# One Trainium2 core, two cross-attention and feed-forward layers: entry into cross attention reordered, opening of linear attention reordered with its row loads in pieces, expert ranks from float16 zeros and ones

## The chip, the cores and the metric

The kernel runs on one core of one Trainium2 chip, in one launch. The metric is the device time of that core in microseconds. Three runs of the kernel before gave 390.52, 391.15 and 392.76 us; their median is 391.15 us. A core has a matrix engine (PE, with its weight load PEld), a vector engine (DVE), a scalar engine (ACT), a general engine (POOL), and SP, which here only issues DMAs. Each works off its own list of instructions in order, and they meet at semaphores. Sums of matmuls stand in PSUM, in eight banks; everything else is in SBUF.

## The reference

Inputs are `x` (32 batches of 64 tokens of 256 numbers: 2048 tokens), a context of the same shape and a mask. Four parts follow each other, each added to `x`:

```python
x = x + _L0_xattn_ref(_layernorm(x), ctx_2048, Wq, Wg, bg, Wkv, Wo)      # linear attention, 16 heads
x = x + _L0_ffn_ref(_layernorm(x), gate_w, ..., se_gate_w)               # 2 of 8 experts, and a shared one
x = x + _L1_xattn_ref(_layernorm(x), ctx_2048, mask, Wq, bq, ..., residual_scale)   # softmax cross attention
x = x + _L1_ffn_ref(_layernorm(x), W0, bias0, W1, bias1)                 # dense feed-forward with gelu
```

Linear attention: `q`, `k` pass through `x+1` or `exp(x)`, `kv_summary = k^T v` and `k_sum` are made per batch and head, and `out = (q kv_summary / (q k_sum) * sigmoid(x Wg + bg)) Wo`. The expert part takes the two best of 8 scores per token, mixes those experts' outputs and adds a gated shared expert. Cross attention makes keys and values of the context, scores, a clipped and masked softmax, the weighted values, an output product and a layer norm of the result.

## The kernel before

The 2048 tokens are 16 tiles of 128. Many products are made from pairs of rounded numbers, a high part (`w0h`, `xTh`, written by ACT) and a low part (`w0l`, `xTl`, the rest, written by DVE or POOL), with three matmuls for one product (`product`, L334 to L336).

**Linear attention** goes in slots, one for a tile, written out by hand for each engine in a `slot0` of its own; an engine's order in a slot is the order of the lines there, and what belongs to other tiles is put in with a distance (`s.tile(2)` is the tile two ahead). On PE a slot holds the key and value product of its tile (L334 to L336, 512 wide), the attention of the tile before (L1924), for even tiles the queries of a pair, the gate product with the bias row (L1990), the product of keys and values (L2004), the transposition of the normed tile two ahead (L375), and the output of the tile two behind. The normed tile comes from ACT (`norm`, L873), which needs the rsqrt that POOL makes for a pair of tiles (`pair_rstd`), which needs the moments that DVE makes (`moments`, L1234 and L1236). Tiles 0 and 1 are normed by DVE ahead of the first slot.

**The opening** is what stands ahead of these slots and slots 0 and 1. SP issues the loads in a written order: rows 0 and 1 of `x` by tiles, the context of tile 0, the layer's weights in pieces (`W0_AT`), the gate's bias, rows of tiles 2 and 3, and so on; the rows of tiles 6 to 15 are one load of 1280 KB. ACT and DVE split each piece of weights (`split_hi`, L840, and `split_w0`, L1189). DVE then writes the two parts of the bias row (`bias_parts`, L1196 and L1198), for which PE's gate product of slot 0 waits, and then the moments of tiles 2 and 3. The expert weights come 482 columns at a time into two buffers in `raw`; ACT rounds them at the end of each slot (`weights_hi_step`, L470), POOL takes the rest (`weights_lo_step`, L482), and the load of piece t waits for POOL's step of piece t - 2.

**Ranks.** A token's place in the list of its expert is its rank among the tokens that chose the expert. For four tiles at a time (`rank_members`, L1897 to L1903) PE multiplies a triangle of ones (`below`) and full squares of ones (`ones`) with `member`, which holds 0 or 1 for each token and expert, all in float32.

**Entry into cross attention.** PE makes keys and values for 8 pairs of context tiles: `keys(p)` and `values(p)`, 12 matmuls each. ACT writes the keys out (`keys`, four instructions, L1027), DVE the values (`values`, L1626), into buffers by head. PE's `values(p)` waits until DVE has written `values(p - 2)`, since they share a bank. Meanwhile POOL fetches the two expert rows of each token (`gather`, L753), two indirect DMAs for a tile; DVE adds them to `x` and takes the moments (`entering`: L1662, L1668, L1675, L1679), POOL makes the rsqrt (`joint_rstd`, L766 to L773), ACT norms (`norm_x`, L1053), PE transposes (L2222) and ACT copies (`normed_in`, L1074). After that come slots again (`slot2`), in which DVE clips scores (`clip`, L1746), then enters the tile four ahead.

Of the kernel before, what the change touches and what calls it, by code (L numbers as in the profile page):

```python
# [20 lines left out]
F16 = mybir.dt.float16  # L21
# [6 lines left out]
P = 128  # L28
# [110 lines left out]
def build(nc, A, out):  # L139
    xs_d = nc.dram_tensor("xs_rows", (XROWS, D), F32, kind="Internal").ap()  # L140
    ys_d = nc.dram_tensor("ys_rows", (USED * P, D), F32, kind="Internal").ap()
    with ExitStack() as ctx:
        def sb(name, shape, dt=F32):
            return ctx.enter_context(nc.sbuf_tensor(name, shape, dt))
# [60 lines left out]
        below, ones = sb("below", [P, P]), sb("ones", [P, P])  # L205
# [46 lines left out]
        member = raw[:, 2020:2148].rearrange("p (t e) -> p t e", e=EXPERTS)  # L252
# [261 lines left out]
        def _(sp):  # L514
# [7 lines left out]
            for i in range(4):  # L522
                load(raw[:, W0_AT[i]:W0_AT[i + 1]], A["w_l0"][:, W0_AT[i]:W0_AT[i + 1]], w0_in[i])
            load(bg_raw[:, :], A["bg"], const_in)
            load(x[:, 2:4, :], x_d[:, 2:4, :], const_in)
# [21 lines left out]
            load(x[:, 6:TILES, :], x_d[:, 6:TILES, :], x_in[1])  # L547
# [8 lines left out]
            with sp.Fori(1, TILES // 2 - 1) as i:  # L556
                for r in range(2):
                    load_ctx(i * 2 + (2 + r), r)
                    load_w(0, i * 2 + r, r)
# [96 lines left out]
        def _(pool):  # L656
# [34 lines left out]
            def slot0(s):  # L691
                if s.is_at(0):
                    pair_rstd(1)
                if tile := s.tile(-3):
                    route_rstd(tile[0])
                if tile := s.tile(2):
                    ctx_lo_step(pool, *tile)
                if s.ring == 1 and s.tile(4):
                    pair_rstd((s.at + 3) // 2)
                if tile := s.tile(-SCATTER_AFTER):  # L700
                    scatter(tile[0])
                if tile := s.tile(0):
                    weights_lo_step(pool, 0, *tile)
# [100 lines left out]
            for t in range(3):  # L804
                gather(t)
            joint_rstd(0)
            gather(3)
            joint_rstd(1)
# [26 lines left out]
        def _(act):  # L835
# [47 lines left out]
            def slot0(s):  # L883
# [20 lines left out]
                if s.is_at(0):  # L904
                    split_hi(4)
# [12 lines left out]
                if s.is_at(0):  # L918
                    ctx_hi_step(act, 2, 0)
                    norm(2)  # L920
# [8 lines left out]
                if tile := s.tile(0):  # L929
                    weights_hi_step(act, 0, *tile)  # L930
# [158 lines left out]
            normed_in(1)  # L1089
            norm_x(2)  # L1090
            keys(6)
# [88 lines left out]
        def _(dve):  # L1180
# [25 lines left out]
            def route_setup(part):  # L1206

                if part == 0:
                    dve.wait_ge(R["weights_hi"], 1)
                    nc.vector.tensor_tensor(rwl, rw_raw[:, :, :], rwh.bitcast(F32),  # L1210
                                            ALU.subtract).then_inc(R["weights"], 1)
                else:
                    dve.wait_ge(late_in, 16 * 6)
                    dve.wait_ge(R["setup"], 4)
                    nc.vector.tensor_scalar(below[:, :], step[:, :], lane[:, 0:1], None, ALU.is_gt)
                    nc.vector.tensor_tensor(upto8[:, :, :], wide(iota8, 2, EXPERTS), wide(iota8, 1, EXPERTS), ALU.is_ge)
# [34 lines left out]
            split_w0(3)  # L1251
            dve.wait_ge(const_in, 16 * 3)
            bias_parts(bg_raw[:, :], 2)
            for t in range(2, 4):
                moments(t)

# [100 lines left out]
            def slot0(s):  # L1357
# [43 lines left out]
                if s.is_at(2):  # L1401
                    dve.wait_ge(x_in[1], 16)
# [296 lines left out]
            ctx_pair_lo(6)  # L1699
            values(2)  # L1700
            entering(0)
            values(3)
            ctx_pair_lo(7)
            entering(1)
            values(4)
# [148 lines left out]
        def _(pe):  # L1854
# [32 lines left out]
            def rank_members(b, scored):  # L1887
# [14 lines left out]
                for t in range(PER_BATCH - 1):  # L1902
                    last = nc.tensor.matmul(  # L1903
                        rank[:, t + 1:, :], ones[:, :],
# [537 lines left out]
```

## Time and profile before

| | us |
|---|---|
| time of the profiled execution | 391.04 |
| its span, from the first instruction to the last | 389.1 |
| PE busy | 367.5 (94%) |
| DVE busy | 293.6 (75%) |
| ACT busy | 244.7 (63%) |
| POOL busy | 219.8 (56%) |

The span is 1.9 us shorter than the time; that part lies ahead of the first and behind the last instruction. A busy PE is not a PE at its peak, since matmuls are pipelined and a matmul that runs at half clock counts as busy too. The mean granted clock of the span is 0.996 of full speed. In the page's 40 slices of 9.7 us PE is busy over 90% in nearly all of them; the first has 7 tenths.

### The profile page before, as it was taken

What the parts mean: (1) busy time and instruction counts of PE and PEld (TensorE: products, weight loads), DVE (VectorE), ACT (ScalarE), POOL (GpSimd) and SP (SyncE); (2) the same over time, 40 slices, a digit from 0 to 9 for tenths busy, and PEclk for the clock granted to TensorE, in tenths of its full rate; (3) what the DMA queues carried; (4) which work ended last, traced back from release to release, by engine and by line L of the source; (5) the groups of instructions that cost most, each with busy time, mean ns of one, the idle gap of its engine ahead of it and who ended that gap; (6) DMA issues with size and microseconds to landing.
All of it is one profiled execution on the core that took longest, in us unless ns stands there. A gap on an engine that the chain in (4) does not pass through costs nothing.

```text
span 389.1 us, 10016 instructions
## 1 busy us (share of the span) xinstructions
PE 367.5 (94%) x3258; PEld 329.5 (85%) x3258; DVE 293.6 (75%) x842; ACT 244.7 (63%) x563; POOL 219.8 (56%) x370
## 2 busy tenths in 40 slices
PE   7799999998999999999999999799999989999996
PEld 6588888786878888989998999688877869999996
DVE  5689988988988879764544499888889995766533
ACT  4576776575554351467876887777877778644550
POOL 3455576378887674604441677577787886531100
PEclk9899999999999999999999999999999999999999
DMA  7561221121332145549784532121120000010101
GB/s 250 187 203 42 79 66 55 40 93 66 87 116 95 70 177 185 161 136 289 232 272 150 192 86 79 50 62 57 54 57 3 2 3 2 7 50 29 56 27 56
DMA packets 31187, 38.13 MB, mean 98 GB/s; under 512 B 4385, under 2 KB 28322, under 8 KB 31138
## 3 DMA queue, kind: packets, MB, share of 16 engines
q1 hardware_dynamic: 28066, 29.11, 24.4%
q0 software_dynamic: 3072, 8.39, 6.4%
q8 instruction: 28, 0.46, 0.5%
q14 instruction: 21, 0.17, 0.1%
HBM read 24.90 MB, written 12.58 MB: 96 GB/s over the span
## 4 chain that ended last, share of the span: by engine, by line
PE 55%; DVE 19%; POOL 12%; issue 8%; ACT 4%; DMA 1%; SPq 0%; ACTq 0%; POOLq 0%; DVEq 0%
PE PS L334 9%; PE PS L335 8%; PE PS L336 8%; PE PS L2266 8%; PE PS L2284 8%; POOL xs_rows L710 3%; PE PS L2101 2%; POOL wfl L482 2%; POOL rj L769 2%; PE PS L2004 2%; ACT raw L1063 1%; POOL rows_early L753 1%; DVE arena_f L1746 1%; PE PS L2342 1%; POOL sj L773 1%
## 5 line engine op out<-in xcount | busy, mean ns | idle before, releaser
L1102 ACT ACTIVATE arena_f<-PS,cols 128x256 f16<-128x256 f32 x64 | 26.5, 472 | 21.6 <-PE PS L2266 19.1
L334 PE MATMUL PS<-wfh,arena_r 128*128 x117 | 35.1, 300 | 2.2 <-DVE arena_r L1602 1.5
L334 PE MATMUL PS<-w0h,arena_r 128*128 128x256 f32 (+1 forms) x96 | 34.8, 363 | 0.6 <-DVE w0l L1189 0.3
L335 PE MATMUL PS<-wfl,arena_r 128*128 x117 | 33.0, 282 | 0.0
L336 PE MATMUL PS<-wfh,arena_r 128*128 x117 | 32.8, 281 | 0.0
L2266 PE MATMUL PS<-arena_r,w1h 128*128 128x256 f32 x128 | 31.2, 284 | 0.0
L335 PE MATMUL PS<-w0l,arena_r 128*128 128x256 f32 (+1 forms) x96 | 31.1, 324 | 0.0
L2266 PE MATMUL PS<-arena_r,w1l 128*128 128x256 f32 x128 | 31.0, 283 | 0.0
L336 PE MATMUL PS<-w0h,arena_r 128*128 128x256 f32 (+1 forms) x96 | 30.9, 322 | 0.0
L488 POOL TENSOR_TENSOR w1l<-raw,w1h 128x384 fp32r<-128x384 f32 (+1 forms) x14 | 12.7, 910 | 29.8 <-ACT w1h L474 29.8
L710 POOL DMA_INDIRECT xs_rows<-rows_early,posi x24 | 24.2, 1010 | 8.9 <-issue 6.7
L1746 DVE TENSOR_SCALAR arena_f<-PS,lim 128x512 f32<-128x512 f32 x32 | 22.4, 743 | 4.4 <-PE PS L2342 4.3
L1608 DVE SCALAR_TENSOR_TENSOR arena_f<-arena_f,PS 128x256 f32<-128x256 f32 x20 | 8.9, 446 | 21.8 <-ACT arena_f L994 21.8
L2266 PEld LDWEIGHTS PS<-arena_r,w1h 128*128 128x128 f32 x128 | 24.5, 191 | 0.4 <-ACT arena_r L1112 0.4
L334 PEld LDWEIGHTS PS<-wfh,arena_r 128*128 128x128 f32 x117 | 22.0, 188 | 3.2 <-issue 3.2
L2266 PEld LDWEIGHTS PS<-arena_r,w1l 128*128 128x128 f32 x128 | 24.5, 191 | 0.0
L335 PEld LDWEIGHTS PS<-wfl,arena_r 128*128 128x128 f32 x117 | 22.1, 189 | 0.0
L336 PEld LDWEIGHTS PS<-wfh,arena_r 128*128 128x128 f32 x117 | 22.0, 188 | 0.0
L334 PEld LDWEIGHTS PS<-w0h,arena_r 128*128 128x128 f32 x96 | 18.4, 191 | 3.9 <-issue 2.1
L482 POOL TENSOR_TENSOR wfl<-raw,wfh 128x482 fp32r<-128x482 f32 (+4 forms) x18 | 19.2, 1070 | 4.3 <-ACT wfh L470 4.1
L1117 ACT ACTIVATE arena_f<-arena_f 128x1024 f32<-128x1024 f32 x16 | 16.9, 1059 | 4.8 <-DVE arena_f L1746 4.8
L336 PEld LDWEIGHTS PS<-w0h,arena_r 128*128 128x128 f32 x96 | 18.3, 191 | 1.5
(317 smaller groups left out, 1375.4 us busy)
## 6 DMA issues: line engine op xcount, KB each, us to landing
arena_f<-xs_rows SPq DMA_DIRECT2D x39, 128.0 KB, 2.5
ys_rows<-raw SPq DMA_DIRECT2D x19, 256.0 KB, 2.9
raw<-in_w_ffn SPq DMA_DIRECT2D x16, 241.0 KB, 2.7
raw<-in_w_l SPq DMA_DIRECT2D x12, 192.0 KB, 3.1
ctx_raw<-in_ctxT SPq DMA_DIRECT2D x16, 128.0 KB, 2.0
out<-arena_f SPq DMA_DIRECT2D x7, 256.0 KB, 2.1
raw<-in_w_l SPq DMA_DIRECT2D x5, 256.0 KB, 4.4
x<-in_x SPq DMA_DIRECT2D x1, 1280.0 KB, 6.4
```

Source lines behind the costliest of these rows:

```text
L334: nc.tensor.matmul(out_ap, lh, rh, start=first, stop=False)
L335: nc.tensor.matmul(out_ap, lh, rl, start=False, stop=False)
L336: return nc.tensor.matmul(out_ap, ll, rh, start=False, stop=last)
L482: last = nc.gpsimd.tensor_tensor(wfl[part][:, to], raw[:, r * FFN_CHUNK + at.start:r * FFN_CHUNK + at.stop], wfh[part][:, to].bitcast(F32) ...
L488: last = nc.gpsimd.tensor_tensor(w1l[:, to], raw[:, r * FFN_CHUNK + first:r * FFN_CHUNK + L1_CHUNK], w1h[:, to].bitcast(F32), ALU.subtract)
L710: nc.gpsimd.indirect_dma_start(out=xs_d, out_offset=bass.IndirectOffsetOnAxis(posi[:, k, t:t + 1], 0), in_=xn2[t % 8], in_offset=None).the ...
L1102: nc.scalar.activation(md16[:, g % 2, n, :], PS[:, M_H[n // 2], (n % 2) * D:(n % 2 + 1) * D], ACT.Gelu, bias=cols[:, 2 * KC + n:2 * KC + n ...
L1117: nc.scalar.activation(flat, flat, ACT.Exp).then_inc(S2["probs"], 1)
L1608: nc.vector.scalar_tensor_tensor(out=gub[:, j % 2, :, :], in0=gub[:, j % 2, :, :], scalar=2.0, in1=up, op0=ALU.mult, op1=ALU.mult).then_in ...
L1746: nc.vector.tensor_scalar(pp[t % 2][:, b, :, :], PS[:, bank:bank + 2, b * 2 * P:(b + 1) * 2 * P], -50.0, lim[:, 2 * t + b:2 * t + b + 1], ...
L2266: last = nc.tensor.matmul(PS[:, M_H[n // 2], (n % 2) * D:(n % 2 + 1) * D], m0w[w][:, c, n * P:(n + 1) * P], mX[g % 2][:, c, :], start=c + ...
L2284: last = nc.tensor.matmul(out, mD[g % 2][:, n, k * P:(k + 1) * P], m1w[w][:, n, :], start=n + w == 0, stop=n + w == NFF)
```

## The change

It has four parts, told here in the order of the program.

1. **Loads.** The load of the rows of tiles 2 and 3 is issued before the third piece of weights instead of behind the bias, and has a semaphore slot of its own. The one load of tiles 6 to 15 becomes three: tiles 6 and 7 in its place, tiles 8 to 11 behind the third piece of expert weights, tiles 12 to 15 behind the fourth.
2. **Order in the opening.** DVE takes the moments of tiles 2 and 3 before it splits the fourth piece of weights and writes the bias. ACT norms tile 2 right after the keys and values of slot 0, before it splits the fifth piece. ACT's and POOL's steps of expert piece 0 move from the end of slot 0 to the end of slot 1, in front of those of piece 1.
3. **Ranks.** `below` and `member` become float16, and there is a float16 copy of `ones` for the products with `member`. The two products with the float32 sums (`carry`, `carry_all`) stay.
4. **Entry.** DVE enters tile 0 before `values(2)`, and tile 1 before `values(3)`. POOL makes tile 0's rsqrt after two gathers instead of three. ACT norms tile 2 behind `keys(6)` instead of before it.

```diff
+                if i == 1:
+                    load(x[:, 2:4, :], x_d[:, 2:4, :], x_in[1])
             load(bg_raw[:, :], A["bg"], const_in)
-            load(x[:, 2:4, :], x_d[:, 2:4, :], const_in)
...
             load_w(0, 0, 0)
-            load(x[:, 6:TILES, :], x_d[:, 6:TILES, :], x_in[1])
+            load(x[:, 6:8, :], x_d[:, 6:8, :], w0_in[4])
             load_w(0, 1, 1)
...
-            with sp.Fori(1, TILES // 2 - 1) as i:
+            for r, (a, b) in enumerate(((8, 12), (12, TILES))):
+                load_ctx(4 + r, r)
+                load_w(0, 2 + r, r)
+                load(x[:, a:b, :], x_d[:, a:b, :], x_in[1 - r])
+
+            with sp.Fori(2, TILES // 2 - 1) as i:
...
-                if tile := s.tile(0):
+                if s.is_at(1):
+                    weights_lo_step(pool, 0, 0, 0)
+                if (tile := s.tile(0)) and s.at:
                     weights_lo_step(pool, 0, *tile)
...
-            for t in range(3):
+            for t in range(2):
                 gather(t)
             joint_rstd(0)
+            gather(2)
+            joint_rstd(1)
             gather(3)
-            joint_rstd(1)
             gather(4)
...
                 if s.is_at(0):
+                    norm(2)
                     split_hi(4)
...
                     ctx_hi_step(act, 2, 0)
-                    norm(2)
...
-                if tile := s.tile(0):
+                if s.is_at(1):
+                    weights_hi_step(act, 0, 0, 0)
+                if (tile := s.tile(0)) and s.at:
                     weights_hi_step(act, 0, *tile)
...
             normed_in(1)
+            keys(6)
             norm_x(2)
-            keys(6)
             queries(0)
...
+                    nc.vector.tensor_copy(ones16[:, :], ones[:, :])
...
             split_w0(2)
-            split_w0(3)
-            dve.wait_ge(const_in, 16 * 3)
-            bias_parts(bg_raw[:, :], 2)
+            dve.wait_ge(x_in[1], 16)
             for t in range(2, 4):
                 moments(t)
+            split_w0(3)
+            dve.wait_ge(const_in, 16 * 2)
+            bias_parts(bg_raw[:, :], 2)
...
             ctx_pair_lo(6)
+            entering(0)
             values(2)
-            entering(0)
-            values(3)
             ctx_pair_lo(7)
             entering(1)
+            values(3)
             values(4)
...
-                        rank[:, t + 1:, :], ones[:, :],
+                        rank[:, t + 1:, :], ones16[:, :],
```

What stands on DVE in the opening, behind the split of the third piece of weights; `w0l` is the low part of the weights, `bias_r` the bias row, `st` and `mvj` the moments. Before:

```order
L1189 TENSOR_TENSOR w0l<-raw,w0h 128x512 x2
L1196 CAST bias_r<-bg_raw 1x256
L1198 TENSOR_TENSOR bias_r<-bg_raw,bias_r 1x256
L1234 BN_STATS st<-x 128x6
L1236 BN_AGGR mvj<-st 128x2
L1234 BN_STATS st<-x 128x6
L1236 BN_AGGR mvj<-st 128x2
```

And now:

```order
L1200 TENSOR_TENSOR w0l<-raw,w0h 128x512
L1246 BN_STATS st<-x 128x6
L1248 BN_AGGR mvj<-st 128x2
L1246 BN_STATS st<-x 128x6
L1248 BN_AGGR mvj<-st 128x2
L1200 TENSOR_TENSOR w0l<-raw,w0h 128x512
L1207 CAST bias_r<-bg_raw 1x256
```

The four moments instructions moved ahead of one split and of the two bias instructions.

What stands on ACT in slot 0, from the writing of the values on; `w0h` is the split of the fifth piece, the two 128x512 rows are the queries, the row from `x,sj,rj` is the norm of tile 2. Before:

```order
L902 ACTIVATE arena_f<-PS 128x2x128
L840 ACTIVATE w0h<-raw 128x512
L916 ACTIVATE arena_f<-PS 128x512
L917 ACTIVATE arena_f<-PS 128x512
L427 ACTIVATE arena_r<-ctx_raw 128x2x128
L873 ACTIVATE arena_f<-x,sj,rj 128x256
L925 ACTIVATE arena_f<-PS 128x256
```

And now:

```order
L911 ACTIVATE arena_f<-PS 128x2x128
L882 ACTIVATE arena_f<-x,sj,rj 128x256
L849 ACTIVATE w0h<-raw 128x512
L926 ACTIVATE arena_f<-PS 128x512
L927 ACTIVATE arena_f<-PS 128x512
L427 ACTIVATE arena_r<-ctx_raw 128x2x128
L934 ACTIVATE arena_f<-PS 128x256
```

The norm moved ahead of the split, the queries and the context step.

What stands on DVE at the entry into cross attention, behind `values(0)` and `values(1)`; a row with `kept_` is one `values(p)`, the rows with `x`, `st` and `mvj` are one `entering`, a row with `arena_r` or `ctx_odd` is a context split. Before:

```order
L1634 TENSOR_TENSOR arena_r<-ctx_raw,arena_r 128x512
L1626 TENSOR_TENSOR kept_w0l<-PS,rows 64x2x8x16 x4
L1662 SCALAR_TENSOR_TENSOR x<-raw,mix,x 128x256
L1668 SCALAR_TENSOR_TENSOR x<-raw,mix,x 128x256
L1675 BN_STATS st<-x 128x6
L1679 BN_AGGR mvj<-st 128x2
L1626 TENSOR_TENSOR kept_w0l<-PS,rows 64x2x8x16 x4
L1634 TENSOR_TENSOR ctx_odd<-arena_f,ctx_odd 128x512
L1662 SCALAR_TENSOR_TENSOR x<-raw,mix,x 128x256
```

And now:

```order
L1651 TENSOR_TENSOR arena_r<-ctx_raw,arena_r 128x512
L1679 SCALAR_TENSOR_TENSOR x<-raw,mix,x 128x256
L1685 SCALAR_TENSOR_TENSOR x<-raw,mix,x 128x256
L1692 BN_STATS st<-x 128x6
L1696 BN_AGGR mvj<-st 128x2
L1643 TENSOR_TENSOR kept_w0l<-PS,rows 64x2x8x16 x4
L1651 TENSOR_TENSOR ctx_odd<-arena_f,ctx_odd 128x512
L1679 SCALAR_TENSOR_TENSOR x<-raw,mix,x 128x256
L1685 SCALAR_TENSOR_TENSOR x<-raw,mix,x 128x256
L1692 BN_STATS st<-x 128x6
L1696 BN_AGGR mvj<-st 128x2
L1643 TENSOR_TENSOR kept_w0l<-PS,rows 64x2x8x16 x4
```

Each of the second and third rows of `values` now stands behind one `entering` more, and the third also behind the second context split.

## Rows read from the trace of the kernel before

**Rows 1.** The page's shares of the chain that ended last, by engine:
```profile
PE 55%; DVE 19%; POOL 12%; issue 8%; ACT 4%; DMA 1%; SPq 0%; ACTq 0%; POOLq 0%; DVEq 0%
```

**Rows 2.** Windows, PE: stretch, its length, PE busy (matmuls), clock, DMA share, GB/s:
```profile
14.10:15.70 1.60, 0.00 (x0) 0.86 0.41 72
15.70:18.60 2.90, 2.89 (x8) 0.50 1.01 347
```

**Rows 3.** Timeline of the opening: start, us, engine, line, instruction [idle before, releaser]:
```profile
9.27 1.28 DVE L1189 TENSOR_TENSOR w0l<-raw,w0h 128x512 fp32r<-128x512 f32 x2
10.47 0.82 DVE L1196 CAST bias_r<-bg_raw 1x256 fp32r<-1x256 f32 x1
...
11.77 0.43 DVE L1234 BATCH_NORM_STATS2 st<-x 128x6 f32<-128x256 f32 x1
11.79 0.60 ACT L916 ACTIVATE arena_f<-PS 128x512 f32<-128x512 f32 x1
...
13.03 0.28 POOL L683 TENSOR_TENSOR vej<-mvj,eps 128x2 f32<-128x2 f32 x1 [1.88 <-DVE mvj L1236]
...
13.78 0.69 DVE L1381 SCALAR_TENSOR_TENSOR arena_f<-arena_f 128x512 f32<-128x512 f32 x1
14.38 0.78 DVE L1389 TENSOR_TENSOR arena_f<-PS,blockmask 128x272 f32<-128x272 f32 x2
...
15.06 0.60 ACT L873 ACTIVATE arena_f<-x,sj,rj 128x256 f32<-128x256 f32 x1 [1.88 <-POOL sj L688]
...
15.71 0.69 PE L375 MATMUL PS<-ident,arena_f 128*128 128x128 f32 x2 [1.66 <-ACT arena_f L873]
...
18.81 0.69 PE L1924 MATMUL PS<-arena_f 128*64 128x136 f32 x8
```

**Rows 4.** Timeline, slot 2: ACT's rounding of expert piece 2:
```profile
27.13 0.62 ACT L470 ACTIVATE wfh<-raw 128x482 fp32r<-128x482 f32 x1
```

**Rows 5.** DMA issues: transfer, queue, count, KB each, us to landing:
```profile
raw<-in_w_ffn SPq DMA_DIRECT2D x16, 241.0 KB, 2.7
...
raw<-ys_rows,posy POOLq DMA_INDIRECT x12, 2.8
```

**Rows 6.** The chain in order of time, start, us, what: pieces in three stages:
```profile
116.21 0.50 PE PS L334
...
135.50 0.14 PE PS L1897 x2
...
135.86 0.65 PE PS L1903 x6
...
324.22 0.22 PE PS L2254 x4
```

**Rows 7.** Timeline: DVE's float32 cast of the same square of ones:
```profile
1.69 0.21 DVE L1204 CAST ones_r<-ones 128x128 fp32r<-128x128 f32 x1
```

**Rows 8.** Timeline of the entry into cross attention, five engines:
```profile
224.10 0.96 POOL L753 DMA_INDIRECT raw<-ys_rows,posy  x1 [0.30 <-issue]
...
225.70 0.69 DVE L1634 TENSOR_TENSOR arena_r<-ctx_raw,arena_r 128x512 fp32r<-128x512 f32 x1
226.49 1.73 DVE L1626 TENSOR_TENSOR kept_w0l<-PS,rows 64x256 f32<-64x256 f32 x4
...
229.97 1.73 DVE L1626 TENSOR_TENSOR kept_w0l<-PS,rows 64x256 f32<-64x256 f32 x4
...
233.63 0.36 PE L334 MATMUL PS<-w1h,arena_r 128*128 128x256 f32 x1
...
243.03 1.73 DVE L1626 TENSOR_TENSOR kept_wfl<-PS,rows 64x256 f32<-64x256 f32 x4 [0.26 <-PE PS L336]
...
243.49 1.16 PE L2342 MATMUL PS<-raw,kept_wfh 64*128 64x128 f32 x16 [0.50 <-ACT raw L1063]
...
248.08 0.19 POOL L766 TENSOR_TENSOR vej<-mvj,eps 128x1 f32<-128x1 f32 x1 [2.75 <-DVE mvj L1679]
...
249.31 0.60 ACT L1053 ACTIVATE arena_f<-x,sj,rj 128x256 f32<-128x256 f32 x1 [1.75 <-POOL sj L773]
```

More of the change, by code:

```diff
@@ L204, in build @@
         lane, step_i, step = sb("lane", [P, 1]), sb("step_i", [P, P], I32), sb("step", [P, P])
-        below, ones = sb("below", [P, P]), sb("ones", [P, P])
+        below, ones16, ones = sb("below", [P, P], F16), sb("ones16", [P, P], F16), sb("ones", [P, P])
         carry, carry_all = sb("carry", [P, EXPERTS]), sb("carry_all", [P, EXPERTS])
@@ L251, in build @@
         picks = raw[:, 1764:2020].rearrange("p (k t e) -> p k t e", k=2, e=EXPERTS)
-        member = raw[:, 2020:2148].rearrange("p (t e) -> p t e", e=EXPERTS)
+        member = raw[:, 2020:2084].bitcast(F16).rearrange("p (t e) -> p t e", e=EXPERTS)
         place = raw[:, 2148:2276].rearrange("p (t e) -> p t e", e=EXPERTS)
@@ L1401, in slot0 @@
                 if s.is_at(2):
-                    dve.wait_ge(x_in[1], 16)
+                    dve.wait_ge(w0_in[4], 16 * 3)
+                if s.is_at(4):
+                    dve.wait_ge(x_in[1], 16 * 2)
+                if s.is_at(8):
+                    dve.wait_ge(x_in[0], 16 * 3)
                 if tile := s.tile(4):
```

## The prediction
> **What bounds the kernel now.** I read the chain that ended last first. PE holds 55% of it and DVE 19%, no DMA to speak of [rows 1]. So PE and whoever keeps PE waiting count, and a transfer counts only where an engine waits for it. Then I went to the three places that the change touches, with the timeline, and asked at each which wait ends last.
>
> In the opening the timeline shows a straight line of waits. DVE splits two pieces of weights (9.27), writes the bias from 10.47 on, and comes to the moments of tile 2 only at 11.77. POOL starts on them at 13.03, ACT norms tile 2 at 15.06, and PE, idle for 1.66 us, transposes it at 15.71 [rows 3]. The second loss is in the windows: PE does nothing from 14.10 to 15.70, and from 15.70 to 18.60 its granted clock is 0.50, which is 1.2 GHz, against 1.00 before [rows 2]. PE gets to the attention of tile 0 only at 18.81 [rows 3].
>
> Ranks: on the chain, the triangle's two records take 0.14 and the six of the squares 0.65, together 0.79 us, for four instructions of the last of four batches [rows 6].
>
> Entry: PE starts the last matmuls of one `values` after the other without a gap, `values(5)` at 233.63, and has only 0.50 us idle (for ACT's queries) before the scores at 243.49. DVE has 0.26 us idle before `values(7)` at 243.03 and clips only after it. What comes behind hangs on DVE: POOL waits 2.75 us for the moments of tile 4 until 248.08, and ACT 1.75 us for POOL until 249.31 [rows 8]. So this stage starts when DVE has written the last values.
>
> **The opening.** I take the new order through slot 0 with the durations of rows 3. DVE's split of piece three ends at 9.27 + 0.64 = 9.9. The moments took 13.03 - 11.77 = 1.26 from their start to POOL's, so POOL starts at about 11.2; from there to ACT's norm it was 15.06 - 13.03 = 2.03, so the norm starts at 13.2 instead of 15.06. The rows of tiles 2 and 3 are there by then: their load now stands one place behind those pieces that DVE splits at 8.3, and one ahead of the piece it splits at 9.27. The price is on ACT: the split of the fifth piece and the two queries, 11.25 to about 12.9 before, now wait behind the norm. Each ACT instruction there has a pitch of about 0.5 to 0.6: norm 13.2, split 13.7, queries 14.3 and 14.8, done at 15.3. DVE's `qq` (0.69) then ends at 16.0 and its masking of the product (0.78) at 16.8, where attention of tile 0 can start. PE gets its gate product later too: split and bias now end at 9.9 + 1.2 + 0.6 + 1.2 = 12.9 in place of 11.75, so PE stands for some 1.2 us before it. But PE is then done with the gate (1.0), the key-value product (0.7), the transposition (0.4) and the next tile's product (1.4 at full clock, for 2.9 it took) at about 16.5. So attention of tile 0 starts at 16.8 instead of 18.81: 2.0 us gained. If the clock falls in the new wait of 1.2 us as it did behind the old one of 1.66, the same list ends at about 17.8 and 1.0 is gained. I take 1.8, since the new wait is the shorter, and keep 0.8 and 2.2 as ends.
>
> Does it last? From slot 2 on I find PE without a gap in nearly every row of the timeline, so what is gained is carried. Further on POOL bounds the stage (from 88 us to 116.21, where PE starts the shared expert when POOL's last split is done [rows 6]), but POOL's run starts from moments that come with the slots, so it moves too. What is new is the load of expert piece 2: it waits for POOL's step of piece 0, which moved behind the moments of tiles 4 and 5. I get that step's end at about 24.2, landing 2.7 us later [rows 5], at 27.0, where ACT, at 27.13 - 1.9 = 25.2 [rows 4], would want it. ACT stands 1.8 us, but it had over 1.5 us idle in slot 3, and PE needs the keys of tile 3 only after its gate product. I cost it at 0 to 0.5 and take 0.1. The other piece loads of `x` are needed slots later; nothing for them.
>
> **The ranks.** The triangle and three squares become four float16 matmuls. The nearest row of such is the float16 transposition, four in 0.22 us [rows 6], also 128x128 in the stationary operand. So 0.79 becomes 0.22, 0.57 saved per batch. Of four batches, the first two lie where DVE or POOL holds the chain, and in the third DVE works on and finds the result waiting. The fourth is on the chain: -0.55, with ends -0.4 (half the records, no faster each) and -1.1 (the third too). The extra cast of ones took 0.21 as a float32 cast [rows 7]; it stands at the end of a DVE slot ahead of PE's next input: +0.1, between 0 and 0.2.
>
> **The entry.** An `entering` costs 229.97 - 226.49 - 1.76 = 1.72 us on DVE, a `values` 1.76 with its gap, a context split 0.75 [rows 8]. In the new order tile 0's rows must be there first. Their second gather is issued at 224.10, landing 2.8 us later [rows 5, 8], at 226.9, while DVE is free at 226.43: it waits 0.5. Then `entering(0)` to 228.65, `values(2)` to 230.4, the split to 231.1, `entering(1)` to 232.85, `values(3)` to 234.6. PE's `values(5)` wants that bank at 233.63 [rows 8] and so stands 0.9 us. `values(4)`, 3.0 us ahead of it in PE's list, wants its bank at 230.6 and just gets it. Nothing else on PE's list has slack but the 0.50 before the scores, so its last values come 0.9 later and DVE's `values(7)` starts at 243.9 instead of 243.03, and with it the clips, tile 4's moments, POOL at 248.08 and ACT's norm at 249.31, all 0.9 later. What the change makes earlier, the norms of tiles 0 and 1, lies in front of nothing: PE reaches their transpositions in its list no sooner. So +0.9, with ends 0 (it can't be negative, as DVE's `values(7)` had only 0.26 of wait before it) and +1.8 (the gathers land 0.9 later).
>
> The DMA page of the Trainium skill (DMA: Bandwidth & Descriptors, Anatomy of one DMA — SWDGE (gpsimd) path) gives such a DMA 2.0 us and its bytes over 436 GB/s. By that page a 128 KB gather would be an estimate of 2.3 us, DVE would not wait, and the entry would cost 0.4 and not 0.9. The trace's median is 2.8, and I go by the trace.
>
> **The sum.** -1.8 + 0.1 - 0.55 + 0.1 + 0.9 = -1.25 us. The profiled execution took 391.04 us (span 389.1 and 1.9 around it), so 389.8 us. The median of the runs shown is 391.15, 0.1 above it; I predict 389.8. A measurement of this kernel tells about 0.5%, 1.96 us, from no change, so the forecast is within it.
>
> **Rivals.**
> - *The entry costs nothing.* The gathers land early, or PE's wait for `values(3)` is short. For it: DVE waits nowhere for a gather in the profile before, so how early they land isn't shown at that place. Against it: even at once landed, `values(3)` ends at 234.1. Then -1.8 + 0.1 - 0.55 + 0.1 = -2.15: 388.9, and with the opening's better end 388.5.
> - *The clock falls in the new waits.* PE's new wait for the bias (1.2 us) or for `values(3)` (0.9 us) brings PE to 1.2 GHz as the 1.66 us did in rows 2, where matmuls that would take 1.4 took 2.9. At the entry PE has no slack: 0.9 + 1.4, and with late gathers 1.8 + 1.4 = 3.2. [...] With only 1.0 from the opening, 0.55 from the ranks and the small terms of 0.2 that is -1.35 + 2.3 to 3.2, or +0.95 to +1.85: 392.0 to 392.9. Slower than before. Against it: gaps under half a microsecond came before the long one in the opening, and the mean of 0.86 in its window says that the clock was still whole at 14.10 [rows 2].
> - *The opening's gain is given back by loads.* ACT stands for expert piece 2 in slot 2 and what is behind it, the transposed tile 4 and the keys of tile 3, comes late to PE; 1.0 to 1.8 of the 1.8 go. Net 0 to +0.5: 391.0 to 391.5. For it: the load now waits for a later step. Against it: ACT's idle time in slot 3.
> - *PE isn't helped by float16.* The records stay at 0.11 us each and only halve; 389.95. It changes little.
>
> **How the numbers follow.** My forecast, between 389.2 and 390.8: 0.47. Entry free: 0.27. Loads eat it: 0.12. Clock falls: 0.14. Most of the entry case is below 389.1, and some of the forecast, which gives 0.34 for faster by over 0.5%; of the clock case 0.06 are above 393.1 and 0.03 for what I don't know, 0.09 for slower; 0.57 within 0.5%. The forecast's own range is 389.2 to 390.8; for 8 in 10 it reaches to 388.1 and 391.8.
>
> **What would show it.** The clock row of 15.7 to 18.6 at 1.00 and the first attention (L1924 before) near 16.8. On ACT, one wait for `in_w_ffn` of up to 1.8 us near 25. One record for each rank matmul, four in about 0.2. At the entry, a DVE wait for `ys_rows` of about 0.5 before the first `x<-raw`, a PE wait of 0.9 for the `kept_` buffer before `values(5)`, and the distance from the first `values` to the first clip 0.9 longer. The prediction is wrong if the distance at the entry is shorter, or if the lead of the opening isn't there at 50 us.

## The result, and the profile after

The changed kernel took 392.13 us (median of 22 runs, 390.99 to 394.55) beside 390.76 for the kernel before (22 runs, 389.79 to 392.76): ratio 1.0041, 95% interval 1.0029 to 1.0054. A second comparison gave 1.0058 (1.0036 to 1.0080). The prediction was 389.8 us, 388.1 to 391.8. It is wrong, and on the other side: 1.4 us slower, not 1.25 faster. Both ratios are within 0.5% or little more of 1, but their intervals leave out 1. The profiled execution took 392.04 us (span 390.2), against 391.04 before.

The experiments ran in five groups, each beside the kernel before. In three of them the kernel before took 403 to 404 us, since DVE and ACT stood there for about 10 us more, in waits whose releaser the profile can't name. I call these the disturbed groups and the other two, with 391 us, the quiet ones. It isn't the chip: the record has chips 3 and 6 in groups of both kinds. The ratios of the disturbed groups are given, but what is read from them rests on distances within the traces.

The page's shares of the chain, after [rows 1]. DMA had 1% of it and now has 4%:

```profile
PE 52%; DVE 17%; POOL 13%; issue 9%; DMA 4%; ACT 3%; SPq 2%; POOLq 0%; ACTq 0%; DVEq 0%
```

The opening, after: two windows, answering [rows 2] (busy time of PE, its weight load, DVE, ACT and POOL, then the granted clock, the DMA share and GB/s), and the timeline that answers [rows 3]:

```profile
12.30:15.20 2.90, 2.57 (x20) 2.25 (x21) 1.30 (x3) 1.86 (x4) 0.91 (x3) 1.00 0.04 14
15.20:18.60 3.40, 2.52 (x20) 1.77 (x18) 3.04 (x10) 2.69 (x9) 1.55 (x2) 1.00 0.70 214
```

```profile
10.10 0.42 DVE L1246 BATCH_NORM_STATS2 st<-x 128x6 f32<-128x256 f32 x1
...
11.35 0.54 POOL L689 TENSOR_TENSOR vej<-mvj,eps 128x2 f32<-128x2 f32 x1 [0.48 <-DVE mvj L1248]
...
12.63 0.36 PE L334 MATMUL PS<-w0h,arena_r 128*128 128x256 f32 x1 [0.64 <-DVE bias_r L1209]
...
13.34 0.60 ACT L882 ACTIVATE arena_f<-x,sj,rj 128x256 f32<-128x256 f32 x1 [2.10 <-POOL sj L694]
...
17.00 0.69 PE L1941 MATMUL PS<-arena_f 128*64 128x136 f32 x8 [0.88 <-DVE arena_f L1402]
```

Up to here the list of the prediction holds: POOL at 11.35 (said 11.2), the norm at 13.34 (13.2), attention of tile 0 at 17.00 (16.8), the clock whole. Then slot 2, after [rows 4]:

```profile
24.59 0.42 ACT L427 ACTIVATE arena_r<-ctx_raw 128x256 fp32r<-128x256 f32 x1 [1.28 <-DMA ctx_raw<-in_ctxT]
...
25.87 0.39 ACT L934 ACTIVATE arena_f<-PS 128x256 f32<-128x256 f32 x1
...
26.40 0.36 PE L334 MATMUL PS<-w0h,arena_r 128*128 128x256 f32 x1 [0.91 <-ACT arena_f L934]
...
26.61 0.61 ACT L470 ACTIVATE wfh<-raw 128x482 fp32r<-128x482 f32 x1 [0.36 <-DMA raw<-in_w_ffn]
```

ACT waits 1.28 us, but for the context of tile 4, which SP issues at 20.37 behind the 640 KB of `rows` (19.90 before); behind it in ACT's list stand the queries and the gate for which PE waits 0.91. Expert piece 2, which I had named, costs 0.36. The lead (how much earlier PE does the same work than in the profile before) falls from 2.2 us at 22 us to 1.1 at 28, and to 0.95 at 48.

Ranks: the chain, after [rows 6], then the first rows of the experts' blocks on PE, after, and the same place before:

```profile
134.50 0.03 PE PS L1914
134.54 0.24 PE PS L1917 x2
134.78 0.06 PE PS L1920 x3
```

```profile
154.36 0.66 PE L2118 MATMUL PS<-ident,arena_f 128*128 128x128 f32 x4 [0.84 <-DMA arena_f<-xs_rows]
...
155.68 0.66 PE L2118 MATMUL PS<-ident,arena_f 128*128 128x128 f32 x4 [0.66 <-DMA arena_f<-xs_rows]
```

```profile
156.31 1.06 PE L2101 MATMUL PS<-ident,arena_f 128*128 128x128 f32 x8 [0.68 <-issue]
```

Four records in about 0.09 us where eight took 0.79: 0.70 saved, the lead is 1.68 at 140 us. But the blocks' rows can be loaded only behind POOL's scatters, 1.27 us each, which go on to 148.4 (148.7 before). PE waits 1.5 us there in place of 0.68, and at 165 us the lead is 1.10. Then PE stands once more, among the blocks; here is the place after, and the same matmul before:

```profile
192.73 0.69 DVE L1619 TENSOR_TENSOR arena_r<-PS,arena_r 128x512 fp32r<-128x512 f32 x1 [0.23 <-ACT arena_r L998]
...
193.80 0.38 PE L334 MATMUL PS<-wfh,arena_r 128*128 x1 [0.81 <-DVE arena_r L1619]
```

```profile
194.19 0.38 PE L334 MATMUL PS<-wfh,arena_r 128*128 x1
```

The lead falls from 1.10 to 0.39 by this wait, and is 0.77 at 215 and 0.70 at 222. DVE, which the profile names, had been done for 0.37 us. The wait goes with the float16 ranks: in all 14 profiles that have them PE stands 0.50 to 0.98 us in front of this matmul, in the 6 without them 0.10 to 0.12. What PE waits for there is not shown.

The entry, after, answering [rows 8]:

```profile
218.43 0.60 ACT L1019 ACTIVATE raw<-PS 128x512 f32<-128x512 f32 x1 [1.07 <-DMA ys_rows<-raw]
...
221.47 3.50 DVE L1643 TENSOR_TENSOR kept_w0h<-PS,rows 64x256 f32<-64x256 f32 x8 [1.19 <-PE PS L336]
...
223.03 1.00 POOL L761 DMA_INDIRECT raw<-ys_rows,posy  x1 [2.73 <-DMA ys_rows<-raw]
...
227.08 0.48 DVE L1679 SCALAR_TENSOR_TENSOR x<-raw,mix,x 128x256 f32<-128x256 f32 x1 [1.38 <-DMA raw<-ys_rows,posy]
...
234.66 0.39 PE L334 MATMUL PS<-w1h,arena_r 128*128 128x256 f32 x1 [0.73 <-DVE kept_w0l L1643]
...
244.08 1.73 DVE L1643 TENSOR_TENSOR kept_wfl<-PS,rows 64x256 f32<-64x256 f32 x4 [0.75 <-PE PS L336]
...
249.14 0.19 POOL L774 TENSOR_TENSOR vej<-mvj,eps 128x1 f32<-128x1 f32 x1 [2.33 <-DVE mvj L1696]
```

DVE waits 1.38 for the gather (predicted 0.5); PE stands 0.51 at `values(4)` (230.58) and 0.73 at `values(5)`; `values(7)`, at 243.03 before, is at 244.08, the first clip at 245.84 in place of 244.79. From there to the end all is 1.05 to 1.1 us later. The chain behind this place is no longer PE's: it is the store of the experts' outputs (`ys_rows<-raw`), POOL's gather, its landing, DVE.

### The profile page after: what moved, and what is told of

The parts are those of the page before. It is cut to its first block, busy times and chain, and to the rows that moved or that the text cites. A ratio compares the mean times of both kernels' runs of the same rounds, so it can differ in the third digit from the quotient of the medians.

```text
span 390.2 us, 9978 instructions
## 1 busy us (share of the span) xinstructions
PE 365.3 (94%) x3242; PEld 326.4 (84%) x3242; DVE 292.1 (75%) x843; ACT 245.1 (63%) x563; POOL 221.0 (57%) x370
## 3 DMA queue, kind: packets, MB, share of 16 engines
q1 hardware_dynamic: 28098, 29.11, 24.2%
## 4 chain that ended last, share of the span: by engine, by line
PE 52%; DVE 17%; POOL 13%; issue 9%; DMA 4%; ACT 3%; SPq 2%; POOLq 0%; ACTq 0%; DVEq 0%
PE PS L2283 8%; PE PS L2301 8%; PE PS L334 8%; PE PS L335 7%; PE PS L336 7%; POOL xs_rows L718 5%; PE PS L2118 2%; DVE arena_f L1763 2%; SPq L516 2%; POOL wfl L482 2%; PE PS L2021 2%; PE PS L2226 1%; PE PS L1876 1%; DMA ys_rows<-raw 1%; POOL rj L777 1%
## 5 line engine op out<-in xcount | busy, mean ns | idle before, releaser
L334 PE MATMUL PS<-w0h,arena_r 128*128 128x256 f32 (+1 forms) x96 | 34.3, 357 | 1.8 <-ACT arena_f L934 0.9
L336 PE MATMUL PS<-w0h,arena_r 128*128 128x256 f32 (+1 forms) x96 | 30.5, 318 | 0.0
```

The lines of the kernel that those rows point to most:

```text
L334: nc.tensor.matmul(out_ap, lh, rh, start=first, stop=False)
L336: return nc.tensor.matmul(out_ap, ll, rh, start=False, stop=last)
```

## The experiments

Three distances tell most. *Lead*: how much earlier PE is than in the profile before, at four times. *Entry*: from DVE's first `values` to its first clip (before: 222.17 to 244.79, 22.62 us). *Gather*: POOL's first gather behind DVE's first `values` (before 222.80, so 0.63).

| kernel | ratio to before (95%) | lead at 48 / 140 / 165 / 222 | gather | entry |
|---|---|---|---|---|
| after | 1.0041 (1.0029-1.0054) | 0.95 / 1.68 / 1.10 / 0.70 | 1.56 | 24.37 |
| after_again | 1.0058 (1.0036-1.0080) | 0.91 / 1.66 / 1.38 / 0.91 | 1.37 | 24.27 |
| entry_only_2 | 1.0052 (1.0034-1.0071) | 1.17 / 1.18 / 1.18 / 0.98 | 0.63 | 24.27 |
| opening_only_3 | 0.9985 (0.9969-1.0000) | 0.81 / 0.86 / 0.89 / 0.45 | 0.60 | 22.62 |
| entry_undone_3 | 1.0032 (1.0011-1.0053) | 0.84 / 1.60 / -0.91 / -1.52 | 1.34 | 23.89 |
| ctx_early_no_entry_2 | 1.0018 (0.9998-1.0038) | 1.68 / 2.36 / 1.48 / 1.37 | 1.46 | 23.89 |
| all_halves_2 | 0.9994 (0.9974-1.0014) | 2.19 / 2.92 / 0.29 / 0.01 | 1.79 | 22.62 |

The distances are of one profiled execution each, and not always a typical one: those of after_again and entry_only_2 took 391.70 and 391.77 us, with medians of 393.50 and 393.35, and that of entry_undone_3 took 395.08, with a median of 392.22.

In the disturbed groups: ranks_only 1.0038 (1.0011-1.0066) and 0.9982 (0.9956-1.0008), entry_only 0.9982 (0.9944-1.0019), entry_undone 1.0021 (0.9988-1.0053) and 1.0007 (0.9972-1.0043), opening_only 0.9949 (0.9911-0.9987) and 0.9959 (0.9931-0.9987), ctx_early 0.9955 (0.9912-0.9997), ctx_early_no_entry 1.0000 (0.9963-1.0037), entry_no_gather_wait 0.9939 (0.9898-0.9980) and 0.9896 (0.9860-0.9932), all_halves 0.9926 (0.9892-0.9960). Two profiles of one kernel differ there by up to 5 us from 136 us on; I read no term of 1 us from these ratios.

**The entry alone**, on the kernel before:

```diff
-            values(2)
             entering(0)
-            values(3)
+            values(2)
             ctx_pair_lo(7)
             entering(1)
+            values(3)
             values(4)
```

(with POOL's `gather(2)` behind `joint_rstd(0)` and ACT's `keys(6)` ahead of `norm_x(2)`, as in the change).

> The kernel before with the new entry order alone. Theory: the gather of tile 0 lands at about 226.85 us there, DVE is free at 226.4, waits 0.4, and values(3) ends 0.8 to 0.9 behind the place where PE wants it: 390.8 + 0.9 = 391.7 us. Without a lead the theory and my prediction's term agree here. Rival: the new order is free without the other edits (the loss is an interaction with them): 390.8.

The first run, in a disturbed group, gave a ratio that tells nothing, but its entry took 24.2 us. Again:

> The kernel before with the new entry alone. Theory: 0.9 to 1.1 us over the kernel before, ratio 1.0025. Rival: 1.000 or less (0.998 in the group before).

1.0052, or 2.0 us, more than the theory had. The trace shows where 1.65 of it comes from:

```profile
221.19 3.50 DVE L1627 TENSOR_TENSOR kept_w0h<-PS,rows 64x256 f32<-64x256 f32 x8 [1.87 <-PE PS L336]
...
223.13 0.96 POOL L753 DMA_INDIRECT raw<-ys_rows,posy  x1 [0.30 <-issue]
...
226.69 0.48 DVE L1663 SCALAR_TENSOR_TENSOR x<-raw,mix,x 128x256 f32<-128x256 f32 x1 [1.28 <-DMA raw<-ys_rows,posy]
...
234.27 0.39 PE L334 MATMUL PS<-w1h,arena_r 128*128 128x256 f32 x1 [0.72 <-DVE kept_w0l L1627]
```

The gather issued at 223.13 lets DVE go at 226.69, 3.56 us later and not 2.8. The profile before had this: its DMA issues, narrowed to that one gather (issued at 224.10), say 3.7:

```profile
raw<-ys_rows,posy POOLq DMA_INDIRECT x1, 3.7
```

In the five profiles with the new entry and its gather DVE gets tile 0's rows 5.4 to 5.6 us behind its first `values`, and is free at 4.2. The wait is 1.2 to 1.4 us in each, and from its end to the clip it is 18.8 us in each. The new entry takes 24.2 to 24.4 us, 1.6 to 1.75 more than 22.62.

**The wait taken away.** Tile 0's two additions read other tiles of `x`; the experts' part of tile 0 is left out.

```diff
-in0=gy[t % RING][:, 0, :]
+in0=(gy[t % RING] if t else x[:, 8:10, :])[:, 0, :]
```

> The changed kernel with the new entry, but the two additions of the experts' rows to tile 0 read two other tiles of x in place of the gathered rows, and DVE's wait for tile 0's gather moves to tile 1, where it is over: the experts' part of tile 0 is left out. The instructions stay. Theory: without the wait of 1.38 us DVE writes values(3) by 233.2, PE at 232.9 hardly waits, and the clips keep the lead: 1.06 + 0.70 - 0.3 = 1.4 less, 390.7 us (ratio to before 1.000). Rival: it isn't the wait but the place of values(3) behind two entering steps that costs (1.0 us of PE's time whatever the gather does): 392.1, ratio 1.0035.

> The changed kernel, but tile 0's experts' part is left out (its two additions read two other tiles of x) and so DVE's wait of 1.3 us for the gather. Theory: from DVE's first values to the first clip 23.0 to 23.2 us in place of 24.3; 1.1 to 1.3 less than the changed kernel, so ratio 1.001 to 1.002 where that one had 1.0041 to 1.0058. Rival: the place of values(3) costs, not the wait: ratio as the changed kernel's.

The entry took 23.08 us in both. The second one's DVE:

```profile
224.41 3.50 DVE L1643 TENSOR_TENSOR kept_w0h<-PS,rows 64x256 f32<-64x256 f32 x8 [1.25 <-PE PS L336]
...
228.54 0.48 DVE L1680 SCALAR_TENSOR_TENSOR x<-x,mix 128x256 f32<-128x256 f32 x1
...
236.10 1.74 DVE L1643 TENSOR_TENSOR kept_wfh<-PS,rows 64x256 f32<-64x256 f32 x4
...
245.73 1.73 DVE L1643 TENSOR_TENSOR kept_wfl<-PS,rows 64x256 f32<-64x256 f32 x4 [0.93 <-PE PS L336]
247.49 1.41 DVE L1764 TENSOR_SCALAR arena_f<-PS,lim 128x512 f32<-128x512 f32 x2
```

So of the 1.65 the wait is 1.2, and 0.45 is the place of `values(3)` (the 0.4 that I had for an entry without a wait). The theory holds by the distance; the ratio was below what it expected, in a group where ratios mean little.

**The entry undone**, in the changed kernel (the old order on DVE, ACT and POOL).

> The changed kernel with the entry into cross attention in the old order (DVE, ACT and POOL). Theory: after the change DVE waits 1.38 us for the gather of tile 0, which hangs on the stores of the experts' outputs and comes no earlier when PE does, so the new order costs the 1.06 us by which the changed kernel is late behind it and the 0.70 us that it was early at 222 us: 1.76. The time is then 392.1 - 1.8 = 390.3 us, 0.4 to 0.5 under the kernel before. First rival, my prediction's own term: the entry costs 0.9 whatever the lead, so 391.2. Second rival: the entry isn't the loss, 391.9 or more.

> The changed kernel with the old entry once more. In the run of this kernel before, code and other transfers that the profile can't name held the engines for 12 us after 144 us, so that its time tells nothing under 0.5%. Theory as there: DVE's wait for tile 0's gather makes the new entry cost 1.76 us, so 390.3 us where the kernel before takes 390.8 and the changed one 392.1 (ratio to before 0.9988). Rival, my prediction's term of 0.9: 391.2 (ratio 1.001). Second rival: the entry isn't the loss: ratio 1.003 or more.

> The changed kernel with the old entry. Theory: 1.8 us less than the changed kernel beside it. Rival, my prediction's term: 0.9 less. Second rival, from the two groups before: nothing less, or more, on a chip that loses 12 us elsewhere.

> The changed kernel as it is, beside the three others of this group on one chip, since the chips of the two groups before took 403 to 404 us for the kernel before and not 390.8. Theory: ratio to the kernel before 1.004, as first measured, if the engines' own waits for code don't hide it. Rival: on such a chip DVE waits 1.7 us at the entry for something that no queue shows (seen in the old order), and the new order's wait for the gather falls into it; then the ratio is 0.998 or less.

Side by side 1.0058 and 1.0032: the old entry gives about 1.0 us back (0.0026 of 391), near my own term and under the theory's 1.8, though the two intervals overlap. The kernel with opening and ranks is still slower than before. That was the surprise. Its entry takes 23.89, not 22.62, though nothing in it differs. The same in the next kernel shows how.

**Tile 4's context sooner**, because of slot 2:

```diff
             load_w(0, 1, 1)
+            load_ctx(4, 0)
             for c in range(KC):
```

> The changed kernel with the load of tile 4's context issued before the router's weights, the small constants and the rows (3.6 us sooner), nothing else. Theory: ACT's 1.28 us wait for it at 23.3 us goes and the attention of tile 2 comes up to 1.1 us earlier. But the entry still waits for the gather, which came no earlier for a lead of 0.7 us, as the last stores hang on older stores (ACT waits 1.07 for one at 218.4): at the end at most half of it, 0.0 to 0.5 under the changed kernel: 391.6 to 392.1, ratio 1.002 to 1.0035. Rival: the whole 1.1 us comes through: 391.0, ratio 1.0006. Second rival, the term of my prediction: ACT then waits for expert piece 2, issued at 23.9 us, and nothing is gained even in slot 2.

> Both: tile 4's context sooner and the old entry. Theory: the clips follow PE's and DVE's lead: 390.3 as for the old entry alone, and up to 1.1 less by the context: 389.3 to 389.9 us, ratio 0.996 to 0.998, the best of these. Rival: the lead of slot 2 is lost at the next transfer anyway: 390.3, ratio 0.9988.

> The old entry with tile 4's context sooner. Theory: 0.4 to 1.1 us less than the changed kernel with the old entry beside it: 1.5 to 2 us less than the kernel before, ratio 0.996. Rival: no less than the old entry alone.

The load is now issued at 16.5 us. ACT no longer waits for the context, and in the profiles of ctx_early and all_halves_2 the lead of 2.4 to 2.5 us at 24 us is 2.2 to 2.4 at 48. (In ctx_early_no_entry_2 it is 1.68 and in ctx_early_no_entry 1.2. There ACT meets the next loads: it waits 2.44 us for expert piece 2 at 27.55 in the one, 1.23 for a context at 30.50 in the other.) In all_halves_2 ACT waits 1.49 us for expert piece 2 instead (26.39), as my prediction had it, and that is indeed hidden; behind the wait of 2.44 us 0.4 of the lead is gone by 33 us. At the end it brings little. Entry of ctx_early_no_entry_2:

```profile
222.26 1.00 POOL L763 DMA_INDIRECT raw<-ys_rows,posy  x1 [2.64 <-DMA ys_rows<-raw]
...
228.67 0.95 POOL L763 DMA_INDIRECT rows_early<-ys_rows,posy  x1 [0.30 <-issue]
229.68 0.19 POOL L776 TENSOR_TENSOR vej<-mvj,eps 128x1 f32<-128x1 f32 x1
...
231.22 0.60 ACT L1065 ACTIVATE arena_f<-x,sj,rj 128x256 f32<-128x256 f32 x1 [1.75 <-POOL sj L783]
...
242.76 1.73 DVE L1644 TENSOR_TENSOR kept_wfl<-PS,rows 64x256 f32<-64x256 f32 x4 [1.38 <-PE PS L336]
244.69 1.41 DVE L1764 TENSOR_SCALAR arena_f<-PS,lim 128x512 f32<-128x512 f32 x2 [0.20 <-PE PS L2360]
```

DVE has tile 0's moments at 228.57, but POOL, which issues six gathers first, begins at 229.68; ACT norms at 231.22 where the kernel before, 1.37 us behind it in all else, did at 231.38. The lead of 1.37 is 0.10 at the clip.

**Ranks alone, opening alone.**

```diff
-                        rank[:, t + 1:, :], ones[:, :],
+                        rank[:, t + 1:, :], ones16[:, :],
```

> The kernel before with float16 ranks alone. My prediction's term: 0.55 saved on PE and 0.1 for the cast, so -0.45: 390.3 us. Rival, from the trace of the changed kernel: PE is 0.7 us further ahead at 136 us, but POOL's 32 scatters, 1.27 us apart, run to 148.4 us whatever PE does, the blocks' rows are loaded only behind them and PE waits for these at 155.6; so nothing is left of it: 390.8.

> The kernel before with float16 ranks alone, on a chip that I hope takes 391 us. Theory now: PE is 0.7 us ahead after the ranks of the last batch, waits for the blocks' rows at 153 us, and with 31 instructions fewer its code is loaded 1.5 us later than before against the stores of the experts' outputs: a store issued about 1 us before such a load lands in 3.7 to 4.1 us, not 2.1, the gathers start 1.2 to 1.5 us behind DVE's first values in place of 0.6, and the old entry waits for POOL. So nothing is gained or 0.3 to 0.8 lost: 391.1 to 391.8 beside 391.0, ratio 1.000 to 1.002. Rival, my prediction's term: -0.45, ratio 0.9988.

> The kernel before with the new opening alone. Theory: of the 2.2 us gained by 21 us, 1.1 go at 24 us, where ACT waits 1.28 us for the context of tile 4, and 0.15 at 44 us; 0.95 stays up to the experts, and 0.7 to 0.95 is left at the end: 389.8 to 390.1 us. Rival, my prediction's term: 1.7 stays, 389.1. Second rival: later waits for transfers (the blocks' rows at 153 us, the stores at 220 us) take all of it: 390.8.

> The kernel before with the new opening alone. Theory: 0.95 to 1.1 us ahead from 24 us on, PE's code loaded as before against the stores (gathers 0.6 us behind the first values), so the old entry keeps nearly all of it: 0.7 to 1.0 under the kernel before where that one's clock falls in the opening, and ratio 0.998. Rival, my prediction's term: 1.7 us, ratio 0.9957. Second rival: the lead is lost at the entry as with ranks and opening together (ratio 1.003): 1.001 or more.

> The new opening alone, once more, for a chip without the 12 us of other waits. Theory: lead of 0.95 to 1.1 us from 24 us on, 0.3 to 1.0 of it left behind the old entry, ratio 0.9975 to 0.999 (the kernel before loses the clock in its opening in only a part of its executions, so its median gains less than its profile). Rival, my prediction's term of 1.7 us: 0.9957. Second rival: nothing left, 1.000 or more.

The opening alone gives 0.9985 (0.6 us less), the same with the ranks 1.0032: the intervals don't touch, though these were two comparisons. The ranks' own ratios contradict each other, and there is no run of them alone in a quiet group. What the traces show is that the gather comes 1.2 to 1.35 us behind the first `values` with ranks alone, 0.60 to 0.63 with the opening alone. The reason is a store. DMA issues and queues, 214.0 to 217.4 us, before, then after:

```profile
q8 instruction: 1, 0.02, 1.8%
issues: line engine op xcount, KB each, median us to landing
ys_rows<-raw SPq DMA_DIRECT2D x2, 256.0 KB, 2.3
arena_f<-in_ctxT SPq DMA_DIRECT2D x1, 256.0 KB, 2.8
```

```profile
q8 instruction: 1, 0.02, 3.3%
issues: line engine op xcount, KB each, median us to landing
ys_rows<-raw SPq DMA_DIRECT2D x2, 256.0 KB, 3.8
arena_f<-in_ctxT SPq DMA_DIRECT2D x1, 256.0 KB, 4.2
```

A load of 16 KB of code takes 1.0 us of one DMA engine before (1.8% of 16 engines for 3.4 us) and starts 0.4 us ahead of a store's issue. After, it starts 0.8 us behind the issue (at 215.1), takes 1.8 us, and the two stores beside it land in 4.1 and 3.5 us where they took 2.1 and 2.5. ACT waits for the buffer (1.07 at 218.43), and all that follows, the last store and the gathers, is later. In the 20 profiles of this study the code load starts 0.8 to 1.3 us behind the issue in 13, and in just these the store lands in 3.2 to 4.2 us; in the other 7 it starts 0.1 to 0.5 ahead, and the store takes 2.1 to 2.3. The 13 all have the float16 ranks, with 32 instructions fewer on PE; of the 7 one has them (entry_undone). That the ranks move the code load is inferred from this, and that the load stretches the store from their going together; neither was tried apart.

**Everything, with gathers in halves.**

```diff
+            for t in range(3):
+                gather(t + 2, [0])
+                joint_rstd(t)
+                gather(t + 2, [1])
```

(opening, tile 4's context sooner, ranks, the old entry on DVE and ACT).

> Opening with tile 4's context sooner, ranks, the old entry on DVE and ACT, and on POOL the two gathers of tiles 2, 3 and 4 parted by the scale step of tiles 0, 1 and 2. Theory: in the old order with a lead ACT's norm of tile 0 comes 8.96 us behind the first gather, since POOL issues six gathers of 1.25 us first; with this order the steps of POOL begin when DVE has the moments, the distance from the first values to the clip falls from 23.9 to 22.6 to 22.9, and the lead of 1.4 us there is kept: ratio 0.9965 to 0.998, the fastest so far. Rival: a gather is then late for DVE (tile 2's or 3's second) and it stays at 1.0018.

> The version with everything: new opening with tile 4's context sooner, ranks, the old entry on DVE and ACT, gathers of tiles 2 to 4 in halves around POOL's scale steps. Theory: 22.6 to 22.9 us from the first values to the clip where the same kernel without halves took 23.9, so 1.0 us under that one (which had ratio 1.0018): 0.9975 to 0.9995, ahead of both kernels. Rival: the halves change nothing on a calm chip: 1.0018.

The entry is back at 22.62 us although the gather is 1.79 late, the latest of all. The halves are the only difference from ctx_early_no_entry_2, whose entry took 23.89. So POOL's six gathers ahead of its scale step were what stretched the old entry, where the gathers are late against DVE. Ratio 0.9994, median 390.16: level with the opening alone (390.18). Both medians are 0.6 under the kernel before beside them (390.81), but both intervals reach 1.0000, so neither is told from no change. The lead was lost elsewhere, at the blocks' rows:

```profile
154.02 0.66 PE L2118 MATMUL PS<-ident,arena_f 128*128 128x128 f32 x4 [1.74 <-DMA arena_f<-xs_rows]
```

```profile
150.60:154.00 3.40, 1.68 (x15) 1.47 (x13) 2.58 (x6) 1.46 (x3) 1.91 (x2) 1.00 0.60 174
154.00:157.40 3.40, 3.16 (x18) 2.93 (x19) 1.26 (x3) 1.20 (x2) 0.00 (x0) 0.72 0.81 238
155.50:158.80 3.30, 3.30 (x18) 3.30 (x17) 2.10 (x4) 0.60 (x1) 0.00 (x0) 0.50 0.79 245
```

PE comes 2.9 us early, stands 1.74, and from 155.5 to 158.8 its clock is 0.50, which is 1.2 GHz: of 2.92 us 0.3 is left.

## Why the prediction was wrong

By the profile the sum was to be -1.25 and is +1.05, the shift of the first clip. Two steps failed above all: the opening's gain was not carried on, and the entry was priced with a gather that lands too soon. The terms:

- **Opening, -1.8 and +0.1 for its loads: -0.95.** The steps of slots 0 and 1 were right within 0.2 us, the first attention too. Wrong was "Does it last? ... what is gained is carried". The load that stopped it was tile 4's context, with the mechanism of my third rival (ACT behind a load in slot 2) on a transfer that I hadn't looked at: SP issued it at about the same time as before, and ACT now came 1.3 us too early. ctx_early shows it: with that load sooner the lead at 28 us is 2.5 in place of 1.1. I should have asked this of all loads of that stretch, not just of those whose wait the change moves. (The rival's own sum was also a little off: -1.25 and 1.0 to 1.8 make -0.25 to +0.55, not 0 to +0.5.)
- **The kernel before wasn't always as in its profile.** In entry_only_2, which has the old opening, PE waits the same 1.66 us as in [rows 3], and the clock stays whole, where [rows 2] have 0.50:

```profile
15.72 0.44 PE L375 MATMUL PS<-ident,arena_f 128*128 128x128 f32 x2 [1.66 <-ACT arena_f L874]
...
17.48 0.69 PE L1925 MATMUL PS<-arena_f 128*64 128x136 f32 x8
```

```profile
15.70:18.60 2.90, 2.88 (x20) 2.16 (x21) 0.76 (x3) 2.13 (x7) 1.24 (x2) 1.00 1.01 345
```

  There the old opening is as far ahead at 48 us (1.17) as the new one. In the two quiet groups 27 of 50 executions of the kernel before had a mean clock of 0.998 or more (medians 390.56 and 390.45 us) and 23 less (391.31 in both). In the five profiles with the old opening the clock falls at 15.1 to 16.4 us in four, in the fifteen with the new one never before 144 us. So a part of what the new opening brings is that its clock doesn't fall. How large a part is open: by the lead of entry_only_2 it would be all, but in the group of opening_only_3 the executions with 0.998 or more are still 0.5 us apart, 389.93 (11 of 12) beside 390.45 (15 of 23).
- **Ranks, -0.55 and +0.1: -0.70 on PE, then nothing.** The size was right, a little small. The step that failed is "the fourth is on the chain": it was on PE's chain, and POOL's scatters, which end 14 us further on, had no slack for it: 0.55 to 0.6 are given back at the blocks' rows. Behind that place they go with the wait of 0.5 to 1.0 us at 193.80 and with the later stores, which the sum had at nothing. So they probably cost.
- **Another 0.4 lost up to 222 us.** The wait at 193.80 takes 0.7, and 0.4 of it comes back by 215. But opening_only_3, without this wait, loses 0.44 over the same stretch, so I can't put the 0.4 down to the ranks.
- **Entry, +0.9: +1.76 (1.65 in entry_only_2).** The mechanism was right, step by step: DVE waits for tile 0's gather, `values(3)` is late for `values(5)`, the clip by as much. The gather's time was mis-sized: I took the page's median of twelve, 2.8 us, where the very gather that DVE would wait for has 3.7 in the same trace. With it the wait is 224.1 + 3.7 - 226.4 = 1.4, and the same list gives 1.8, my upper end ("the gathers land 0.9 later"). In the changed kernel this gather lands in 2.7, but the gathers start 0.9 later against DVE; that the wait is the same 1.4 is a coincidence. And I took the gather as fixed against DVE's start, while it hangs on stores: a lead that does not reach them makes DVE wait the longer.

-0.95 - 0.70 + 0.55 + 0.4 + 1.76 = +1.06.

The rival that the clock falls in the new waits (for the bias or for `values(3)`) did not happen in the profile (waits of 0.64, 0.88, 0.91, 0.51 and 0.73 us at clock 1.00), nor in those two places in any other profile with the new opening or the new entry. That the measured 392.13 lies in its range, 392.0 to 392.9, is luck. (Its 0.06 above 393.1 also lie outside that range.) The clock may fall elsewhere in some executions: seven of the 22 had a mean clock of 0.996 or less and took 393.3 to 394.6, the others 391.0 to 392.7. By the DMA rule that the prediction set beside the trace (the Trainium skill, DMA: Bandwidth & Descriptors, Anatomy of one DMA, SWDGE path) the gather would take an estimate of 2.3 us; the traces have 2.7 to 3.8, so the rule was further off than the median.

Not settled: what the ranks cost alone in a quiet group, what PE waits for at 193.80, what the nameless waits of 10 us are, and what exactly takes the 0.4 us between 165 and 222.

## What to carry to other kernels

A gain on the engine that bounds a kernel lasts only up to the next place where it meets a chain that it doesn't drive: follow each stretch behind the gain, and list for each transfer when it is issued and by whom, not just the waits that one sees, since the early engine makes new ones. For a DMA that nobody waited for so far, read the landing of that very transfer; a median over the kernel hides what happens beside it. And before a wait is priced by a fallen clock in one profile, look at how many executions show that clock.

## What the hardware showed that I had not expected

- The same wait of PE, 1.66 us at 15.7 us, is followed by half clock in the profile before and by full clock in entry_only_2. Of waits at the blocks' rows, 0.84 + 0.66 us and 1.08 + 0.70 (ctx_early_no_entry_2) left the clock whole; 1.00 + 0.85 (entry_undone_3) and 1.74 + 0.22 (all_halves_2) were followed by 3.4 us at 1.2 GHz.
- Where a 16 KB load of code starts amid a 256 KB store, the store takes 3.2 to 4.2 us in place of 2.1 to 2.3 (13 and 7 profiles), the next up to 3.8 in place of about 2.5, and the code load up to 1.8 in place of 1.0. So removing instructions can probably, by moving such loads, change a time at a far place.
- The gathers show the same: the first four take 2.7 to 3.0 us as a rule, but in all eight quiet profiles one that was issued 1.0 to 1.6 us ahead of a code load takes 3.5 to 3.8 (before: issued at 224.10, code load at 225.56; entry_only_2: 223.13 and 224.50). Two more took 3.6 where a code load started 2.7 and 2.8 us behind their issue. The cause is inferred here too.
- A float16 matmul of 0 and 1 with 8 to 32 columns takes 0.02 to 0.03 us of PE's chain, a float32 one 0.07 to 0.11 for each of its two records [rows 6].
